# Quantising the second FFN's input in 512-column slices, shared between VectorE and ScalarE and interleaved in program order with the output matmuls

## The chip, the cores and the metric

The kernel runs on the 8 cores of one Trainium2 chip. Each core takes one of the 8 sequences of the batch, with the same weights, and the cores don't talk to each other. The metric is the device time of the slowest core in microseconds. The engines that matter here are TensorE (PE in the rows), VectorE (DVE), ScalarE (ACT) and SyncE (SP), which only issues DMAs. ScalarE issues DMAs too (ACTq).

## The reference, cut to what matters

One layer: a selective-scan attention substitute, a layernorm, a feed-forward net with quantised activations and ternary weights, and another layernorm. Per core, sequence length 2048, model width 2048, hidden width 8192.

```python
def _act_quant(x):
    scale = QB / jnp.maximum(jnp.max(jnp.abs(x), axis=-1, keepdims=True), EPS)   # QB = 127
    q = jnp.clip(jnp.round(x * scale), -QB - 1, QB) / scale
    ...
def _bitlinear(x, w):
    return jnp.einsum('bsd,od->bso', _act_quant(x), _weight_quant(w))
...
gv = _bitlinear(h, w_gv)
value, gate = jnp.split(gv, 2, axis=-1)
u = value * jax.nn.silu(gate)
out = _bitlinear(u, w_out)
return residual + out
```

The change is about the step `_act_quant(u)`: each of the 8192 x 2048 values of u is multiplied by its token's scale and rounded to an integer of at most 127 in size. The scale needs the maximum over all 8192 hidden channels, so rounding can begin only when all of u is there.

## The kernel before

Activations lie with channels on the 128 partitions and tokens along the free dimension: a hidden chunk `j` (of `HC` = 64) is a tile of 128 x 2048, and `ts` (of `NTS` = 4) names a slice of `TS` = 512 tokens. The program runs in stages, one after the other: the scan, the mean of the weights, the first layernorm and quantisation (token slices of 512), the first FFN matmul with u as its result (u goes to DRAM as `u_sp`, f32), the ternary `w_out` (to DRAM as `qo_sp`, bf16), then the two stages that the change touches.

**Quantising u (lines 1140 to 1202, "Q2" below).** A loop over the 64 chunks, whole tiles of 128 x 2048. SyncE loads `u_sp[j]` (1 MB) into one of two halves of `ub`, and waits before each load until chunk j-2 is finished (`tok_q2f`), so the next chunk's load runs under the current chunk. VectorE multiplies by the scale `s2b`; ScalarE takes Sign and Abs; VectorE peels the rounded size bit by bit (`emit_peel`, line 53: seven times a comparison into `tq` and a subtraction from `rq`), then one multiplication and one subtraction give the integer `q2t` in bf16. ScalarE's queue stores it to `q2_sp` in DRAM.

**The output matmul and layernorm ("F2" below, from line 1245).** A loop over the four token slices. SyncE first waits that all of q2 is stored, then loads per step `qo_r` (256 KB) and `q_r` (`q2_r`, 128 KB) into rings of four; TensorE runs 2 x 64 steps of 8 matmuls (line 1286) into all of PSUM; ScalarE copies the results to `o_ts`; SyncE loads the residual `lbuf` (16 DMAs); then comes a tail: VectorE scales and adds (two passes over 128 x 8192), TensorE and ScalarE make the layernorm's sums, VectorE the statistics, ScalarE copies the broadcast mean and 1/std (`tok_bc6c`), VectorE makes two more passes over 128 x 8192 (`tok_out`), and ScalarE's queue stores 16 pieces to `outT`. The next slice's matmuls wait for `tok_bc6c` only, so they run beside the last two passes and the stores.

**What sets the order.** Each engine, SyncE included, executes its own instructions strictly in the order in which the program emits them. Each compute instruction of VectorE and ScalarE is followed by a wait of that engine for its own result; dependences on others are further waits placed before the instruction. A wait holds up all that is behind it on the same engine:

```python
def call(*a, **kw):
    r = f(*a, **kw)
    s.inc(r)
    e.wait_ge(s.h, s.n)
    return r
```

## Time and profile before

| | us |
|---|---|
| median of the 2 timed runs (8724.84 and 8746.99) | 8735.91 |
| the profiled execution | 8729.62 |
| span of its slowest core, core 0, first to last instruction | 8728.1 |
| spans of the 8 cores | 8684.9 to 8728.1 |
| VectorE busy | 4400.0 (50%) |
| TensorE busy | 3306.6 (38%) |
| ScalarE busy | 2212.0 (25%) |

The profile is of one execution, on its slowest core. All times within it count from that core's first instruction. An engine's busy share is an average over stages with different limits, so it says little by itself. The stages can be told apart by time: Q2 runs from 5006 to about 7417 us, F2 from there to the end at 8728 us. "Idle before, releaser" in a row is the time that the engine stood still before the instruction and what ended that.

### The profile page before, as it was taken

The numbers are of one execution on the slowest core, as the hardware profiler recorded it, in microseconds if no ns is written. First come the engines' busy times: TensorE is split into PE (matmuls) and PEld (weight loads), VectorE is DVE, ScalarE is ACT, GpSimd is POOL, SyncE is SP. The second block draws the span as 40 slices with busy tenths as digits, with TensorE's granted clock in tenths as the row PEclk, the third lists the DMA queues.
The fourth block names the chain that finished last, engine by engine and source line by source line (L and its number), as shares of the span: only waits on it lengthen the run. The fifth ranks groups of instructions, "written<-read, shape, count | busy, mean of one in ns | idle before, by whom it ended". The sixth has DMA issues, their size and how long they took to land.

```text
span 8728.1 us, 45431 instructions; the slowest of 8 cores (8684.9 to 8728.1 us)
## 1 busy us (share of the span) xinstructions
PE 3306.6 (38%) x13138; PEld 1338.2 (15%) x13138; DVE 4400.0 (50%) x2983; ACT 2212.0 (25%) x2199; POOL 44.1 (1%) x87
## 2 busy tenths in 40 slices
PE   2100102102399988898820000000000000977966
PEld 0000000000144433333310000000000000422422
DVE  4500174674644444444433488888888888011011
ACT  3544323123234343343455401111011110001010
POOL 1000000000000000000000000000000000000000
PEclk7555555555688899999965555555555555988988
DMA  7775301001122222222245301111111110755754
GB/s 172 268 255 187 116 19 39 27 12 36 58 92 97 92 102 92 97 97 92 102 147 200 134 36 43 43 43 43 38 42 43 43 43 35 216 172 161 218 165 147
DMA packets 316760, 887.05 MB, mean 102 GB/s; under 512 B 43872, under 2 KB 109408, under 8 KB 267360
## 3 DMA queue, kind: packets, MB, share of 16 engines
q1 hardware_dynamic: 249264, 704.77, 25.3%
q10 hardware_dynamic: 55296, 167.80, 4.9%
q0 software_dynamic: 11952, 11.57, 1.0%
q8 instruction: 107, 1.75, 0.1%
q14 instruction: 141, 1.16, 0.0%
HBM read 727.79 MB, written 167.77 MB: 103 GB/s over the span
## 4 chain that ended last, share of the span: by engine, by line
DVE 44%; PE 19%; ACT 19%; DMA 11%; issue 4%; ACTq 1%; DVEq 1%; SPq 1%; POOL 0%; POOLq 0%
DVE rq L80 12%; PE pout L1286 9%; DVE tq L80 8%; DMA wmean<-wgvt 4%; PE pvg L1012 4%; PE pvg L1017 4%; ACT wqt L80 4%; ACT wqs L80 4%; DMA wmean<-woutT 3%; DVE res L80 3%; DVE paby L80 3%; ACT wabs L80 2%; DMA q_r<-q_sp 2%; DVE Mx L80 2%; DVE ub L80 2%
## 5 line engine op out<-in xcount | busy, mean ns | idle before, releaser
L1286 PE MATMUL pout<-q_r,qo_r 128*128 128x512 bf16 x4096 | 919.7, 387 | 2492.1 <-DMA q_r<-q_sp 2455.1
L1012 PE MATMUL pvg<-q,qwv 128*128 128x512 bf16 x4096 | 1056.4, 417 | 308.9 <-DVE qwg L80 159.1
L80 DVE TENSOR_TENSOR rq<-rq,tq 128x2048 f32<-128x2048 f32 x448 | 1027.0, 2292 | 48.1 <-DVE tq L80 1.8
L1017 PE MATMUL pvg<-q,qwg 128*128 128x512 bf16 x4096 | 984.1, 396 | 0.0
L1286 PEld LDWEIGHTS pout<-q_r,qo_r 128*128 128x128 bf16 x4096 | 403.3, 99 | 3012.8 <-issue 2559.9
L80 DVE TENSOR_SCALAR tq<-rq 128x2048 f32<-128x2048 f32 x448 | 549.6, 1227 | 309.4 <-ACT rq L80 268.0
L80 ACT ACTIVATE sgq<-ub 128x2048 bf16<-128x2048 f32 x64 | 122.2, 1909 | 2118.3 <-DVE ub L80 2118.3
L1012 PEld LDWEIGHTS pvg<-q,qwv 128*128 128x128 bf16 x4096 | 428.6, 105 | 902.0 <-issue 615.0
L80 ACT ACT_TABLE_LOAD x78 | 100.1, 1283 | 1753.3 <-PE pout L1286 536.5
L80 DVE TENSOR_TENSOR o_ts<-o_ts,c2b 128x8192 f32<-128x8192 f32 x4 | 34.8, 8691 | 985.6 <-DMA lbuf<-ln_sp 985.6
L80 ACT ACTIVATE wabs<-wmean 128x2048 f32<-128x2048 f32 (+1 forms) x256 | 379.6, 1483 | 457.6 <-DMA wmean<-wgvt 245.2
L1017 PEld LDWEIGHTS pvg<-q,qwg 128*128 128x128 bf16 x4096 | 414.2, 101 | 527.5 <-issue 189.6
L80 DVE SCALAR_TENSOR_TENSOR qo_t<-wqt,wqs 128x1024 bf16<-128x1024 f32 x128 | 156.9, 1226 | 345.3 <-ACT wqs L80 345.3
L80 DVE TENSOR_REDUCE redW<-accW 128x1 f32<-128x128 f32 x2 | 0.6, 286 | 643.8 <-ACT wabs L80 643.7
L80 ACT ACTIVATE wqt<-wld,sgv 128x2048 f32<-128x2048 f32 x128 | 256.3, 2002 | 251.3 <-DVE qwv L80 163.8
L80 DVE SCALAR_TENSOR_TENSOR qwv<-wqt,wqs 128x2048 bf16<-128x2048 f32 x64 | 146.7, 2292 | 312.8 <-ACT wqs L80 308.0
L80 ACT ACTIVATE sg_t<-gc_t 128x512 f32<-128x512 f32 x256 | 161.2, 630 | 564.2 <-DVE gc_t L80 564.2
L80 DVE SCALAR_TENSOR_TENSOR qwg<-wqt,wqs 128x2048 bf16<-128x2048 f32 x64 | 146.7, 2292 | 275.6 <-ACT wqs L80 275.6
L80 DVE TENSOR_TENSOR Mx<-Mx,au_t 128x512 f32<-128x512 f32 x256 | 177.2, 692 | 213.4 <-ACT au_t L80 213.4
L80 DVE TENSOR_TENSOR sg_t<-sg_t,c1b 128x512 f32<-128x512 f32 x256 | 177.2, 692 | 211.9 <-ACT sg_t L80 211.9
L80 ACT ACTIVATE au_t<-u_r 128x512 f32<-128x512 f32 x256 | 161.2, 630 | 469.5 <-DVE u_r L80 469.5
L80 ACT ACTIVATE wqs<-wld,sgv 128x2048 bf16<-128x2048 f32 x128 | 256.2, 2002 | 12.4 <-ACT wqt L80 0.8
(141 smaller groups left out, 3349.1 us busy)
## 6 DMA issues: line engine op xcount, KB each, us to landing
wmean<-wgvt SPq DMA_DIRECT2D x128, 1024.0 KB, 5.6
wld<-wgvt SPq DMA_DIRECT2D x128, 1024.0 KB, 5.2
qo_r<-qo_sp SPq DMA_DIRECT2D x512, 256.0 KB, 3.1
wmean<-woutT SPq DMA_DIRECT2D x128, 512.0 KB, 4.3
u_sp<-u_r ACTq DMA_DIRECT2D x64, 1024.0 KB, 3.8
wo_r<-woutT SPq DMA_DIRECT2D x128, 512.0 KB, 3.5
ub<-u_sp SPq DMA_DIRECT2D x64, 1024.0 KB, 4.7
q_r<-q_sp SPq DMA_DIRECT2D x512, 128.0 KB, 3.6
```

The costliest lines, as they stand in the source:

```text
L80: r = f(*a, **kw)
L1012: t.matmul(pvg[:, 2 * q * TS:(2 * q + 1) * TS], qwv[:, r * 2048 + k * 128:r * 2048 + (k + 1) * 128], q1[:, (ts * DC + k) * TS:(ts * DC + k ...
L1017: last = t.matmul(pvg[:, (2 * q + 1) * TS:(2 * q + 2) * TS], qwg[:, r * 2048 + k * 128:r * 2048 + (k + 1) * 128], q1[:, (ts * DC + k) * TS ...
L1286: last = t.matmul(pout[:, d * TS:(d + 1) * TS], qo_r[:, (i % 4) * 1024 + d * 128:(i % 4) * 1024 + (d + 1) * 128], q2_r[:, (i % 4) * TS:(i ...
```

## The change

The stage Q2 over whole chunks is taken out. In its place `emit_q2_slice(ts)` quantises one slice of 512 tokens, all 64 chunks of it, and the body of the F2 loop becomes `emit_f2_slice(ts)`. The program emits them in the order q2(0), q2(1), f2(0), q2(2), f2(1), q2(3), f2(2), f2(3), and every engine's instructions stand in this order.

Within q2(ts) two chunks are worked on together as two lanes. Each has one half of `ub2`, `zt2`, `mq2` and `q2c` (128 x 512 each). VectorE multiplies each lane by the scale; then there are eight levels k, in each of which ScalarE takes the Sign of the remainder plus 0.5 (`bias=pbh[:]`, a tile of 128 x 1) and VectorE adds `HYB_S[k]` times that sign to the remainder (`scalar_tensor_tensor`). A last `scalar_tensor_tensor` per lane gives the integer plus 0.5, ScalarE subtracts 0.5 and converts to bf16 (Copy), and its queue stores 128 KB to `q2_sp`. `vfin[nj]` is the count of VectorE's last instruction on a lane; the load of the chunk two further on, into the same half of `ub2`, waits for it. In F2, SyncE waits for the stores of this slice instead of all (`rQ2S`), and for a list of events `BND` of earlier stages. The diff, cut:

```diff
--- before.py
+++ after.py
     c2b = sb(nc.sbuf_tensor("c2b", [128, S], F32))
+    s2b = sb(nc.sbuf_tensor("s2b", [128, S], F32))
+    pbh = sb(nc.sbuf_tensor("pbh", [128, 1], F32))
+    pbm = sb(nc.sbuf_tensor("pbm", [128, 1], F32))
...
-    ub = f15.enter_context(nc.sbuf_tensor("ub", [128, 2 * S], F32))
-    rq = f15.enter_context(nc.sbuf_tensor("rq", [128, S], F32))
-    tq = f15.enter_context(nc.sbuf_tensor("tq", [128, S], F32))
-    sgq = f15.enter_context(nc.sbuf_tensor("sgq", [128, S], BF16))
-    q2t = f15.enter_context(nc.sbuf_tensor("q2t", [128, 2 * S], BF16))
...
-    @blk.sync
-    def _(s):
-        for j in range(HC):
-            s.wait_ge(*TOK[("usp", j)])
-            if j < 2:
-                s.wait_ge(sV.h, tok_s2row)
-                s.wait_ge(sA.h, tok_c2b)
-                for h_, v_ in tok_qosp:
-                    s.wait_ge(h_, v_)
-            else:
-                s.wait_ge(sV.h, tok_q2f(j - 2))
-            ub_toks[j] = rUB.inc(j, s.dma_start(out=ub[:, (j % 2) * S:(j % 2 + 1) * S],
-                                                in_=u_sp[j]))
-
-    @SCA
-    def _(sc):
-        for j in range(HC + 1):
-            if j < HC:
-                sc.wait_ge(sV.h, tok_q2y(j))
-                if j >= 1:
-                    sc.wait_ge(sV.h, tok_q2f(j - 1))
-                sc.activation(out=sgq[:], in_=ub[:, (j % 2) * S:(j % 2 + 1) * S],
-                              func=AF.Sign)
-                sc.activation(out=rq[:], in_=ub[:, (j % 2) * S:(j % 2 + 1) * S],
-                              func=AF.Abs)
-            if j >= 1:
-                jj = j - 1
-                sc.wait_ge(sV.h, tok_q2f(jj))
-                rQ2S.inc(jj, sc.dma_start(out=q2_sp[jj],
-                                          in_=q2t[:, (jj % 2) * S:(jj % 2 + 1) * S]))
-    tok_q2abs_end = sA.n
-    @VEC
-    def _(v):
-        v.wait_ge(sA.h, tok_c2b)
-        for j in range(HC):
-            r = j % 2
-            v.wait_ge(*ub_toks[j])
-            v.tensor_mul(out=ub[:, r * S:(r + 1) * S],
-                         in0=ub[:, r * S:(r + 1) * S], in1=s2b[:])
-            v.wait_ge(sA.h, q2_a0 + 2 * (j + 1))
-            emit_peel(v, rq[:], tq[:])
-            v.tensor_mul(out=tq[:], in0=rq[:], in1=sgq[:])
-            if j >= 2:
-                v.wait_ge(rQ2S.sems[j % 2].h, 16 * (j // 2))
-            v.tensor_sub(out=q2t[:, r * S:(r + 1) * S],
-                         in0=ub[:, r * S:(r + 1) * S], in1=tq[:])
-    assert sV.n == q2_v0 + 17 * HC, (sV.n, q2_v0)
-
-    tok_q2sp = [s.tok() for s in rQ2S.sems]
...
+    ub2 = f2b(nc.sbuf_tensor("ub2", [128, 2 * TS], F32))
+    zt2 = f2b(nc.sbuf_tensor("zt2", [128, 2 * TS], F32))
+    mq2 = f2b(nc.sbuf_tensor("mq2", [128, 2 * TS], F32))
+    q2c = f2b(nc.sbuf_tensor("q2c", [128, 2 * TS], BF16))
...
+    HYB_S = [-64.0, -32.0, -16.0, -8.0, -4.0, -2.0, -1.0, -0.5]
+
+    BND = ([(sV.h, tok_s2row), (sV.h, tok_qodone), (sA.h, tok_woq),
+            (sA.h, tok_c2b), (sLn1.h, tok_ln1_all)]
+           + [TOK[("usp", HC - 2)], TOK[("usp", HC - 1)]] + list(tok_qosp))
+
+    vfin = {}
+    ub2_toks = {}
+    q2stash = {}
+
+    def emit_q2_slice(ts):
+        vb, ab = sV.n, sA.n
+        for jj in range(HC):
+            vfin[ts * HC + jj] = vb + 20 * (jj // 2) + 19 + (jj % 2)
+        sl = slice(ts * TS, (ts + 1) * TS)
+
+        @blk.sync
+        def _(s, ts=ts):
+            for jj in range(HC):
+                nj = ts * HC + jj
+                if ts == 0:
+                    s.wait_ge(*TOK[("usp", jj)])
+                    if jj < 2:
+                        for h_, v_ in BND:
+                            s.wait_ge(h_, v_)
+                if nj >= 2:
+                    s.wait_ge(sV.h, vfin[nj - 2])
+                r = jj % 2
+                ub2_toks[nj] = rUB.inc(nj, s.dma_start(
+                    out=ub2[:, r * TS:(r + 1) * TS],
+                    in_=u_sp[jj, :, ts * TS:(ts + 1) * TS]))
+
+        @VEC
+        def _(v, ts=ts, vb=vb, ab=ab, sl=sl):
+            for pj in range(HC // 2):
+                for lane in range(2):
+                    jj = 2 * pj + lane
+                    v.wait_ge(*ub2_toks[ts * HC + jj])
+                    r = jj % 2
+                    v.tensor_mul(out=ub2[:, r * TS:(r + 1) * TS],
+                                 in0=ub2[:, r * TS:(r + 1) * TS],
+                                 in1=s2b[:, sl])
+                for k in range(8):
+                    for lane in range(2):
+                        r = (2 * pj + lane) % 2
+                        v.wait_ge(sA.h, ab + 18 * pj + 2 * k + lane + 1)
+                        v.scalar_tensor_tensor(
+                            out=zt2[:, r * TS:(r + 1) * TS],
+                            in0=mq2[:, r * TS:(r + 1) * TS], scalar=HYB_S[k],
+                            in1=(ub2 if k == 0 else zt2)[:, r * TS:(r + 1) * TS],
+                            op0=ALU.mult, op1=ALU.add)
+                for lane in range(2):
+                    r = (2 * pj + lane) % 2
+                    v.scalar_tensor_tensor(
+                        out=mq2[:, r * TS:(r + 1) * TS],
+                        in0=zt2[:, r * TS:(r + 1) * TS], scalar=-1.0,
+                        in1=ub2[:, r * TS:(r + 1) * TS],
+                        op0=ALU.mult, op1=ALU.add)
+        assert sV.n == vb + 20 * (HC // 2)
+
+        @SCA
+        def _(sc, ts=ts, vb=vb, ab=ab):
+            for pj in range(HC // 2):
+                for k in range(8):
+                    for lane in range(2):
+                        r = (2 * pj + lane) % 2
+                        sc.wait_ge(sV.h, vb + 20 * pj
+                                   + (1 + lane if k == 0 else 2 * k + 1 + lane))
+                        sc.activation(out=mq2[:, r * TS:(r + 1) * TS],
+                                      in_=(ub2 if k == 0 else zt2)[:, r * TS:(r + 1) * TS],
+                                      func=AF.Sign, bias=pbh[:])
+                for lane in range(2):
+                    jj = 2 * pj + lane
+                    nj = ts * HC + jj
+                    r = jj % 2
+                    sc.wait_ge(sV.h, vfin[nj])
+                    if nj >= 2:
+                        sc.wait_ge(*q2stash[nj - 2])
+                    sc.activation(out=q2c[:, r * TS:(r + 1) * TS],
+                                  in_=mq2[:, r * TS:(r + 1) * TS],
+                                  func=AF.Copy, bias=-0.5)
+                    q2stash[nj] = rQ2S.inc(r, sc.dma_start(
+                        out=q2_sp[jj, :, ts * TS:(ts + 1) * TS],
+                        in_=q2c[:, r * TS:(r + 1) * TS]))
+        assert sA.n == ab + 18 * (HC // 2)
 
...
+    def emit_f2_slice(ts):
...
-            for h_, v_ in tok_q2sp:
-                s.wait_ge(h_, v_)
+            for l_ in range(2):
+                s.wait_ge(rQ2S.sems[l_].h, 16 * (HC // 2) * (ts + 1))
             for h_, v_ in tok_qosp:
                 s.wait_ge(h_, v_)
+            if ts == 0:
+                for h_, v_ in BND:
+                    s.wait_ge(h_, v_)
             for dg in range(2):
                 for j in range(HC):
...
             if prev_next_ok is not None:
                 t.wait_ge(sA.h, prev_next_ok)
+            else:
+                t.wait_ge(sA.h, tok_c2b)
...
+    emit_q2_slice(0)
+    for ts in range(NTS):
+        if ts + 1 < NTS:
+            emit_q2_slice(ts + 1)
+        emit_f2_slice(ts)
```

## Rows read from the trace of the kernel before

**Rows 1.** Windows: length; busy of PE, PEld, DVE, ACT, POOL; clock; DMA share; GB/s.

```profile
5006.00:7420.00 2414.00, 0.00 (x0) 0.00 (x0) 2016.56 (x1088) 245.68 (x130) 0.00 (x0) 0.50 0.11 42
7420.00:7655.00 235.00, 226.13 (x1023) 100.23 (x1024) 0.00 (x0) 5.96 (x9) 0.00 (x0) 0.98 0.77 215
7728.00:7976.00 248.00, 231.57 (x1022) 101.39 (x1023) 17.38 (x2) 6.05 (x10) 0.00 (x0) 0.95 0.75 217
```

**Rows 2.** Groups of instructions by shape: busy us, mean ns; idle before, releasers.

```profile
L80 DVE TENSOR_TENSOR rq<-rq,tq 128x2048 f32<-128x2048 f32 x448 | 1027.0, 2292 | 48.1 <-DVE tq L80 1.8
...
L80 DVE TENSOR_SCALAR tq<-rq 128x2048 f32<-128x2048 f32 x448 | 549.6, 1227 | 309.4 <-ACT rq L80 268.0 <-DVE rq L80 0.9
...
L80 DVE SCALAR_TENSOR_TENSOR qwg<-wqt,wqs 128x2048 bf16<-128x2048 f32 x64 | 146.7, 2292 | 275.6 <-ACT wqs L80 275.6
```

**Rows 3.** Instructions on tile ub: duration min/median/max, first and last start.

```profile
L80 DVE TENSOR_TENSOR ub<-ub,s2b x64: 2291/2292/2293, 5011.1 to 7377.0; 128x2048 f32<-128x2048 f32 x64
```

**Rows 4.** SyncE's waits: for what, us in total, times, longest.

```profile
SPq L1162 <- DVE q2t L80: 2304.0, 62, 42.4
```

**Rows 5.** Timeline (start, us, engine), SyncE first to F2's matmuls, final passes and stores.

```profile
5006.22 43.80 SPq L1163 DMA_DIRECT2D ub<-u_sp  x3
...
7420.15 20.22 PE L1286 MATMUL pout<-q_r,qo_r 128*128 128x512 bf16 x85 [2417.36 <-DMA q_r<-q_sp]
...
7728.34 23.90 PE L1286 MATMUL pout<-q_r,qo_r 128*128 128x512 bf16 x96 [2.89 <-ACT rstd2b L80]
...
7736.99 8.69 DVE L80 TENSOR_TENSOR o_ts<-o_ts,rstd2b 128x8192 f32<-128x8192 f32 x1
...
7745.76 14.12 ACTq L1431 DMA_DIRECT2D outT<-o_ts  x16
...
8373.54 2.72 PE L1286 MATMUL pout<-q_r,qo_r 128*128 128x512 bf16 x6 [2.89 <-ACT rstd2b L80]
```

**Rows 6.** Groups by shape, 512 columns; the third has a 1-column tile as bias.

```profile
L80 DVE TENSOR_TENSOR Mx<-Mx,au_t 128x512 f32<-128x512 f32 x256 | 177.2, 692 | 213.4 <-ACT au_t L80 213.4
...
L80 ACT ACTIVATE au_t<-u_r 128x512 f32<-128x512 f32 x256 | 161.2, 630 | 469.5 <-DVE u_r L80 469.5
...
L80 ACT ACTIVATE scr<-scr,epsc 1x512 f32<-1x512 f32 x12 | 8.6, 720 | 0.1
```

**Rows 7.** Timeline, a two-buffer exchange between ScalarE and VectorE in the first quantisation.

```profile
1157.00 0.63 ACT L80 ACTIVATE paby<-hbuf 128x512 f32<-128x512 f32 x1 [0.23 <-DVE m1t L80]
1157.08 0.69 DVE L80 TENSOR_TENSOR m1t<-m1t,paby 128x512 f32<-128x512 f32 x1 [0.17 <-DVE m1t L80]
1157.86 0.63 ACT L80 ACTIVATE paby<-hbuf 128x512 f32<-128x512 f32 x1 [0.23 <-DVE m1t L80]
```

**Rows 8.** Timeline, ScalarE alone: copies without a further wait, squares with one.

```profile
7656.58 4.62 ACT L80 COPY o_ts<-pout 128x512 f32<-128x512 f32 x7 [0.37 <-ACT o_ts L80]
...
7701.44 10.72 ACT L80 ACTIVATE sqb<-o_ts 128x512 bf16<-128x512 f32 x14 [14.21 <-PE pout L1376]
```

**Rows 9.** Timeline, additions whose two-buffer loads wait for the addition two before.

```profile
1001.99 0.69 DVE L80 TENSOR_TENSOR res<-res,xr 128x512 f32<-128x512 f32 x1 [2.39 <-DMA xr<-xT]
...
1005.85 0.69 DVE L80 TENSOR_TENSOR res<-res,xr 128x512 f32<-128x512 f32 x1 [2.23 <-DMA xr<-xT]
```

**Rows 10.** Tile xr: time from issue to landing of its 64 loads.

```profile
DMA to landing us min/median/max: 2.6/3.0/4.1
```

**Rows 11.** DMA issues: line, engine, count, KB each, median us to landing.

```profile
ub<-u_sp SPq DMA_DIRECT2D x64, 1024.0 KB, 4.7
...
xr<-xT SPq DMA_DIRECT2D x64, 256.0 KB, 3.0
```

**Rows 12.** Timeline of ScalarE: 16 stores, then the next block's table load and work.

```profile
1091.55 9.02 ACTq L677 DMA_DIRECT2D ln_sp<-res  x16
1100.60 1.28 ACT L80 ACT_TABLE_LOAD   x1 [26.72 <-issue]
1101.90 2.13 ACT L80 ACTIVATE sqb<-res 128x512 bf16<-128x512 f32 x3
```

**Rows 13.** Timeline of ScalarE: a copying instruction followed by Silu in one block.

```profile
94.70 0.59 ACT L80 CAST zbf<-pz 128x512 bf16<-128x512 f32 x1 [2.87 <-DVE zf L80]
97.36 0.60 ACT L80 ACTIVATE gsil<-pg 128x512 f32<-128x512 f32 x1 [2.08 <-PE pg L259]
```

More of the change, by code:

```diff
@@ L239, in _ @@
         v.memset(yacc[:], 0.0)
+        v.memset(pbh[:], 0.5)
+        v.memset(pbm[:], -0.5)
     tok_init = sV.n
@@ L1250, in build_program @@
     prev_mm_end = None
-    for ts in range(NTS):
+    def emit_f2_slice(ts):
+        nonlocal prev_next_ok, prev_res2, prev_mm_end
         f2_m0 = sMM.n
@@ L1307, in _ @@
             s.wait_ge(sLn1.h, tok_ln1_all)
+            if ts == 0:
+                for h_, v_ in BND:
+                    s.wait_ge(h_, v_)
             if prev_res2 is not None:
```

31 lines of the change are left out of this document (removed).

## The prediction

> **What bounds the kernel now.** I read the windows first. They cut the time that the change touches in two. In Q2, 2414 us, TensorE does nothing at all, VectorE is busy 2017 us and ScalarE 246 us. In a slice of F2 it is the reverse: 226 of 235 us are TensorE's, in the first slice, and the granted clock is 0.98 (2.4 GHz) where Q2 had 0.50 (1.2 GHz) [rows 1]. So Q2 is VectorE's stage. Its groups by shape say what fills it: seven comparisons of 1.23 us and seven subtractions of 2.29 us per chunk, and three more passes of 2.29 us [rows 2]. The 64 chunks follow each other every (7377.0 - 5011.1) / 63 = 37.55 us [rows 3]. SyncE's waits show that no load is late there: SyncE waits 2304 us in total for VectorE to free a buffer, never the other way round in the steady state [rows 4]. After Q2 comes F2, four times in turn. The first matmul of slice 0 starts at 7420.15, that of slice 1 at 7728.34, that of slice 3 at 8373.54, and the span ends at 8728.1 [rows 5].
>
> **Does anything overlap after the change?** The emission order q2(1), f2(0), q2(2), f2(1), q2(3), f2(2), f2(3) looks as if q2(ts+1) ran beside f2(ts). Follow SyncE, which keeps its order. The loads of f2(0) stand behind the 64 loads of q2(1), and each of these waits for the chunk two before it (`vfin`). So f2(0)'s matmuls get their first data when the last pair of q2(1) has been loaded. In return q2(2) is behind f2(0)'s whole tail on VectorE and on ScalarE. The two stages still alternate; only the last of the 32 pairs of q2(1), q2(2) and q2(3) lies beside the following matmuls. The question is therefore what 32 pairs cost against 16 old chunks, 16 x 37.55 = 601 us.
>
> **One pair, step by step.** VectorE has 20 passes of 512 columns, at 0.692 us each [rows 6]; the `scalar_tensor_tensor` costs as much as the plain multiplication at 2048 columns, 2292 ns [rows 2], so I take 0.692 for it too. ScalarE has 16 Signs at 0.72 us (0.630 for an ACTIVATE, 0.720 for one with a column as bias) and 2 Copies at 0.63 [rows 6]. What lies between instructions decides as much. The exchange paby/m1t has this very pattern, two buffers, each engine waiting for itself and for the other: VectorE repeats every 0.86 us, which is 0.69 and a gap of 0.17 [rows 7]. The hand-over from VectorE to ScalarE takes 0.09 (1157.77 to 1157.86). ScalarE with only its own wait has a gap of (4.62 - 7 x 0.585) / 6 = 0.09, and with one more wait, already fulfilled, (10.72 - 14 x 0.63) / 13 = 0.14 [rows 8]. A level then costs:
> - ScalarE: 2 x (0.72 + 0.14) = 1.73 us;
> - VectorE: 2 x (0.69 + 0.17) = 1.72 us;
> - one lane's own chain: 0.72 + 0.10 + 0.69 + 0.09 = 1.61 us.
>
> The dearest rules: 1.73, a value that the chain bounds from below (1.61) and the gap of 0.23 that ScalarE shows in the exchange [rows 7] from above (1.90). A pair from its first multiplication: that one and the hand-over 0.79; seven levels 12.1; then the last Sign of lane 1, 0.86 + 0.72, hand-over 0.10, VectorE's last level step 0.69, gap 0.10 and the final pass of lane 0, 0.69. Together 16.05 us. Only now may lane 0's next load go, since both halves of `ub2` are in use: the prefetch that Q2 had is gone. The additions `res<-res,xr` show the price of such a loop with loads of the same shape (256 KB, rows of 2 KB): an addition ends at 1002.68 and the one that needs the freed buffer starts at 1005.85 [rows 9], 3.17 us, of which landing is 3.0 (2.6 to 4.1) [rows 10]. So a pair takes 16.05 + 3.17 = 19.2 us. ScalarE's Copies and its two DMA issues fall into these 3.2 us and the next multiplication: 2 x (0.63 + 0.33) and gaps are 2.3 us, out of 4.0. If that cover were gone they would cost up to 2.3 us a pair.
>
> A slice is 32 x 19.2 = 614 us against 601 before: VectorE's work fell (20 x 0.692 = 13.8 us a pair, 443 us a slice, against 2017 / 4 = 504), but the levels alternate at ScalarE's pace and the load lies bare.
>
> The Trainium skill, in "DMA: Bandwidth & Descriptors", section "Anatomy of one DMA", gives a fixed 2.0 us plus the bytes at 436 GB/s. By that rule, which speaks against cutting 1 MB loads into bare 256 KB ones, a load is an estimated 2.6 us and the total 50 us less than mine. The rows have 3.0 for 256 KB and 4.7 for 1 MB [rows 11], so they decide, and the 2.6 agrees with the smallest landing.
>
> **The sum, in the trace's time.**
> - q2(0) starts as Q2 did, SyncE at 5006.2 [rows 5]; with 3.2 for the load, the first multiplication is at 5009.4.
> - 63 pairs, to the start of the last pair of q2(1): 1209.6. Each block of ScalarE begins with a table load of 1.28 us [rows 12], two of them: 2.6. Now 6221.6.
> - f2(0)'s loads are issued behind lane 1's last load, some 2 us before this, and need 3 to 4 us: first matmul 1.8 later, 6223.4.
> - f2(0) from first matmul to the end of the fourth pass on VectorE, as before: 7745.68 - 7420.15 = 325.5 [rows 5]. Now 6548.9.
> - q2(2) cannot start its Signs then: ScalarE first issues 16 stores, and in front of the same pattern of the first layernorm 9.0 us of issues and 1.3 of table load went by [rows 12]. Against the normal hand-over that is 9.6 us. Then 31 pairs, 595.2: 7153.7.
> - f2(1): 1.8 + 325.5. q2(3): 9.6 + 595.2. First matmul of f2(2) 1.8 later: 8087.6.
> - f2(2) to f2(3)'s first matmul: 308.2, as slice 0 [rows 5]. The old slices 1 to 3 began beside the stores of `outT` (248 us for slice 1's matmuls against 235 [rows 1]); in f2(1) and f2(2) that contention goes. The low clock at their start is already in slice 0's 308.2, since it too followed an idle TensorE.
> - f2(3) as before: 8728.1 - 8373.5 = 354.6. Span 8750.
>
> That is 22 us, 0.25%, above the span of before. The sum is against that execution (8729.6 us); carried to the median of the runs, 8735.9 x 8750 / 8728.1 = 8758 us. The gains (most of a pair hidden three times, 3 x 17.4 = 52 us; two slices without contention, 645.2 - 2 x 308.2 = 29) are eaten by the quantising itself, 128 pairs and their starts against 2414, 49 us, and by passes and stores that no longer lie beside matmuls, 2 x (17.3 + 9.6) = 54.
>
> **Rivals.** Two per cent of 8736 us is 175 us, about what a measurement of this kernel can tell from no change. With 128 pairs that is 1.2 us a pair above mine for slower, and 1.5 below for faster.
> 1. The second wait is hidden and loads land at their quickest. Then the lane's chain rules, 1.61 a level, and loads take 2.6: 0.9 + 0.4 = 1.3 us a pair, -166: 8592. For it: the two engines are within 0.12 us a level of it. Against it: the gap of 0.17 stands in each step of the exchange, with both waits fulfilled [rows 7]. Chance 8%, with half-way cases.
> 2. Slower: Sign and Copy don't share a table, so ScalarE loads one before the first Copy and one before the next pair's first Sign. The first is covered by the load of u, the second comes after the multiplication that it waits for: 1.28 us bare, and little slack left, 165 us: 8923. It decides on slower from 1.2 us a pair. Against it: a copying instruction is followed by Silu without a load in one block [rows 13], and Sign, Abs and Silu alternate in the FFN stage. For it: the new Copy is an ACTIVATE with a bias, which the trace never shows. Chance 5%. The page "ScalarE: Activation LUTs" of the Trainium skill, section "Table sets: the hidden batching unit", has copy among the cheap functions in every set, which speaks against this rival too; that these rows agree for Silu is all that the trace bears out.
> 3. Dearer: the loads of u suffer from the stores beside them and from the other cores and land after up to 4.1 us, the longest of xr [rows 10], or ScalarE's gap is 0.23 as in the exchange [rows 7] and not 0.14. That is up to 1.1 us a pair for the one, 8899, and up to 2 x 8 x 0.09 = 1.4 for the other, 8938; both in full, 9080. Against it: the 0.23 there is ScalarE waiting for a slower partner, and here it is the slower one. Chance 15%, half of it beyond 2%.
> 4. The overlap works after all and three slices' matmuls vanish under quantising: 3 x 235 = 705, 8053. Against it stands SyncE's order, which nothing in the diff breaks. Chance 2%.
>
> The forecast itself: 70%. The likeliest's 8758 is the predicted time. The range 8660 to 8900 leaves out rivals 2 and 4, most of 1 and the far half of 3, about 2 in 10 in all. Faster by over 2%: 2% from rival 4 and 3% from rival 1 with cheaper passes. Slower by over 2%: rival 2 with 5% and 8% of rival 3. Within 2%: 82%.
>
> **What the profile after would show.** Starts of the multiplication on `ub` every 19.2 us within q2; per level two Signs of 0.72 and two VectorE passes of 0.69 in 1.73 us; about 3.1 us of VectorE idle before each pair, released by DMA; TensorE idle for about 580 us three times and busy in four blocks of 235 us, the first starting near 6223; no table loads inside a block. Wrong would be my pair if the Sign with a bias is dearer than 0.72 or the load dearer than 3.2, and the frame if matmuls run beside more than one pair.

## The result and the profile after

| | before | after |
|---|---|---|
| median (us), lowest to highest | 8744.5, 8711.6 to 8848.8 | 8907.4, 8878.2 to 9041.9 |
| executions | 10 | 11 |
| ratio of times, 95% interval | | 1.019, 1.0156 to 1.0225 |
| span of core 0 in the profiled execution | 8728.1 | 8875.9 |

The kernel became slower by 163 us, seven times the 22 us of the forecast. The time lies just above the range (8900) and 1.9% above before; the interval of the ratio reaches past 2%, so it isn't settled whether the loss is more or less than 2%. The sign is the one of the sum. The ratio leaves out executions in which one die ran at a lower clock and took longer, such as the one of 9041.9; the medians and the extremes are those of all. The account below goes by core 0, the core whose rows the prediction rests on.

First the frame. Timeline of TensorE on core 0 after (start, us, engine, operation, idle before): the first matmuls of the four F2 slices.

```profile
6292.49 1.01 PE L1294 MATMUL pout<-q_r,qo_r 128*128 128x512 bf16 x2 [1278.64 <-ACT mq L80]
...
7254.91 1.44 PE L1294 MATMUL pout<-q_r,qo_r 128*128 128x512 bf16 x3 [657.19 <-ACT mq L80]
...
8218.28 1.01 PE L1294 MATMUL pout<-q_r,qo_r 128*128 128x512 bf16 x2 [658.72 <-DMA q_r<-q_sp]
...
8528.31 1.01 PE L1294 MATMUL pout<-q_r,qo_r 128*128 128x512 bf16 x2 [2.89 <-ACT rstd2b L80]
```

TensorE is idle before the first matmul for 1279 us (from the stage ahead on, so this holds q2(0) and q2(1)) and before the second and third for 657 and 659 us. The windows of core 0 (columns as in [rows 1]) say the same in another way: 388 us in the middle of q2(2), then the matmuls of f2(0), f2(1) and f2(2).

```profile
6862.00:7250.00 388.00, 0.00 (x0) 0.00 (x0) 266.61 (x386) 246.56 (x347) 0.00 (x0) 0.50 0.14 39
...
6292.00:6530.00 238.00, 226.39 (x1023) 100.29 (x1024) 12.31 (x18) 17.83 (x26) 0.00 (x0) 0.97 0.75 215
7254.90:7492.90 238.00, 226.43 (x1024) 100.30 (x1024) 11.76 (x17) 18.16 (x27) 0.00 (x0) 0.98 0.74 216
8218.00:8456.00 238.00, 227.50 (x1023) 100.34 (x1024) 12.28 (x18) 17.79 (x26) 0.00 (x0) 0.97 0.75 214
```

In the matmuls' 238 us VectorE is busy for 12 us: 17 or 18 passes, the rest of one pair. Nothing else of q2 overlaps. SyncE's waits (core 5, the slowest) say who holds the order together: it spends 2617.5 us waiting for the final passes before it may load the next chunk.

```profile
SPq L1189 <- DVE mq L80: 2617.5, 248, 114.6
```

Then the pair. Tile `ub` on core 0 (its multiplications from first to last, what the engines' idle time before its instructions ended with, and the landing of its loads):

```profile
L80 DVE TENSOR_TENSOR ub<-ub,s2b x256: 691/692/695, 5020.5 to 8217.0; 128x512 f32<-128x512 f32 x128
...
  DMA ub<-u_sp: 421.6, 248
...
DMA to landing us min/median/max: 3.0/3.5/7.7
```

One pair of core 0, timeline, from the multiplication of its lane 0 to that of the next pair:

```profile
5081.94 0.69 DVE L80 TENSOR_TENSOR ub<-ub,s2b 128x512 f32<-128x512 f32 x1 [2.78 <-DMA ub<-u_sp]
5082.72 0.72 ACT L80 ACTIVATE mq<-ub,pbh 128x512 f32<-128x512 f32 x1 [2.36 <-DVE ub L80]
5083.06 0.69 DVE L80 TENSOR_TENSOR ub<-ub,s2b 128x512 f32<-128x512 f32 x1 [0.43 <-DMA ub<-u_sp]
...
5084.71 12.02 ACT L80 ACTIVATE mq<-zt,pbh 128x512 f32<-128x512 f32 x14
...
5085.65 0.69 DVE L80 SCALAR_TENSOR_TENSOR zt<-mq,zt 128x512 f32<-128x512 f32 x1 [0.17 <-DVE zt L80]
5086.51 0.69 DVE L80 SCALAR_TENSOR_TENSOR zt<-mq,zt 128x512 f32<-128x512 f32 x1 [0.17 <-DVE zt L80]
...
5097.68 1.49 DVE L80 SCALAR_TENSOR_TENSOR mq<-zt,ub 128x512 f32<-128x512 f32 x2
5098.45 1.11 SPq L1191 DMA_DIRECT2D ub<-u_sp  x2
5098.52 0.63 ACT L80 ACTIVATE q2c<-mq 128x512 bf16<-128x512 f32 x1 [1.78 <-DVE mq L80]
5099.22 0.35 ACTq L1244 DMA_DIRECT2D q_sp<-q2c  x1
5099.73 0.63 ACT L80 ACTIVATE q2c<-mq 128x512 bf16<-128x512 f32 x1 [0.59 <-DVE mq L80]
5100.44 0.33 ACTq L1244 DMA_DIRECT2D q_sp<-q2c  x1
5101.85 0.69 DVE L80 TENSOR_TENSOR ub<-ub,s2b 128x512 f32<-128x512 f32 x1 [2.69 <-DMA ub<-u_sp]
```

The pair takes 5101.85 - 5081.94 = 19.91 us. Lane 1's multiplication begins 1.12 us after lane 0's, released by its own load and not by lane 0's end (that would be 0.86). The passes repeat every 0.865. The final pass of lane 0 ends at 5098.37, the load is issued at 5098.45, and 3.48 us after the freed buffer the next multiplication starts. Over the pairs of core 0 inside slices (without the first pairs of q2(2) and q2(3), whose Signs start 10 us late behind the stores) the mean is 20.14 us a pair, of which 3.60 are from the freed buffer to the multiplication, with lane 1 on average 1.06 behind lane 0. The other cores have 20.15 to 20.24.

Groups of the page after, core 5 (busy us, mean ns; idle before, releaser), and at the end the page's count of instruction fetches (packets, MB):

```profile
L80 ACT ACTIVATE mq<-zt,pbh 128x512 f32<-128x512 f32 x1792 | 1293.5, 722 | 280.6 <-DVE zt L80 24.5
L80 DVE SCALAR_TENSOR_TENSOR zt<-mq,zt 128x512 f32<-128x512 f32 x1792 | 1242.0, 693 | 325.6 <-DVE zt L80 258.5
...
L80 ACT ACT_TABLE_LOAD x81 | 103.9, 1283 | 1743.1 <-PE pout L1294 469.4
...
L80 DVE TENSOR_TENSOR ub<-ub,s2b 128x512 f32<-128x512 f32 x256 | 177.2, 692 | 434.3 <-DMA ub<-u_sp 433.3
...
L80 ACT ACTIVATE q2c<-mq 128x512 bf16<-128x512 f32 x256 | 161.3, 630 | 309.5 <-DVE mq L80 307.8
...
q14 instruction: 237, 1.94, 0.1%
```

The Sign with a column as bias takes 722 ns, the scaled addition 693, the Copy 630: the three durations that the prediction took from other instructions [rows 6] hold to 3 ns. The table loads went from 78 to 81, one for each of the three blocks that ScalarE has more; none stands inside a block.

### The profile page after: what moved, and what is told of

Same layout as the page of the kernel before. It is cut to its first block, busy times and chain, and to the rows that moved or that the text cites. A ratio compares the mean times of both kernels' runs of the same rounds, so it can differ in the third digit from the quotient of the medians.

```text
span 8963.6 us, 57819 instructions; the slowest of 8 cores (8839.0 to 8963.6 us)
## 1 busy us (share of the span) xinstructions
PE 3331.3 (37%) x13138; PEld 1344.3 (15%) x13138; DVE 4158.0 (46%) x4457; ACT 3611.0 (40%) x4378; POOL 44.1 (0%) x87
## 4 chain that ended last, share of the span: by engine, by line
DVE 39%; ACT 21%; DMA 15%; PE 13%; issue 7%; DVEq 1%; ACTq 1%; SPq 1%; POOL 0%; POOLq 0%
DVE zt L80 13%; PE pout L1294 10%; DMA ub<-u_sp 5%; ACT wqt L80 4%; ACT wqs L80 4%; DMA wmean<-wgvt 4%; ACT mq L80 3%; DMA wmean<-woutT 3%; DVE res L80 3%; DVE paby L80 3%; DVE Mx L80 2%; ACT wabs L80 2%; DVE sg_t L80 2%; DVE gc_t L80 2%; DVE u_r L80 2%
## 5 line engine op out<-in xcount | busy, mean ns | idle before, releaser
L1294 PE MATMUL pout<-q_r,qo_r 128*128 128x512 bf16 x4096 | 1004.1, 413 | 2653.3 <-DMA q_r<-q_sp 2622.4
L80 ACT ACTIVATE mq<-zt,pbh 128x512 f32<-128x512 f32 x1792 | 1293.5, 722 | 280.6 <-DVE zt L80 24.5
L80 DVE SCALAR_TENSOR_TENSOR zt<-mq,zt 128x512 f32<-128x512 f32 x1792 | 1242.0, 693 | 325.6 <-DVE zt L80 258.5
L1016 PE MATMUL pvg<-q,qwv 128*128 128x512 bf16 x4096 | 1030.8, 410 | 367.3 <-DVE u_r L80 206.7
L1021 PE MATMUL pvg<-q,qwg 128*128 128x512 bf16 x4096 | 941.6, 384 | 0.0
L1294 PEld LDWEIGHTS pout<-q_r,qo_r 128*128 128x128 bf16 x4096 | 425.6, 104 | 3236.0 <-issue 3007.4
L80 DVE TENSOR_TENSOR ub<-ub,s2b 128x512 f32<-128x512 f32 x256 | 177.2, 692 | 434.3 <-DMA ub<-u_sp 433.3
L80 ACT ACTIVATE mq<-ub,pbh 128x512 f32<-128x512 f32 x256 | 184.7, 722 | 350.2 <-DVE ub L80 349.1
L80 ACT ACTIVATE q2c<-mq 128x512 bf16<-128x512 f32 x256 | 161.3, 630 | 309.5 <-DVE mq L80 307.8
```

The costliest lines, as they stand in the source:

```text
L1016: t.matmul(pvg[:, 2 * q * TS:(2 * q + 1) * TS], qwv[:, r * 2048 + k * 128:r * 2048 + (k + 1) * 128], q1[:, (ts * DC + k) * TS:(ts * DC + k ...
L1021: last = t.matmul(pvg[:, (2 * q + 1) * TS:(2 * q + 2) * TS], qwg[:, r * 2048 + k * 128:r * 2048 + (k + 1) * 128], q1[:, (ts * DC + k) * TS ...
L1294: last = t.matmul(pout[:, d * TS:(d + 1) * TS], qo_r[:, (i % 4) * 1024 + d * 128:(i % 4) * 1024 + (d + 1) * 128], q2_r[:, (i % 4) * TS:(i ...
```

## The sum against the trace, step by step

| step, core 0 | forecast (us) | measured | difference |
|---|---|---|---|
| start of the first multiplication | 5009.4 | 5020.5 | +11.1 |
| from there to f2(0)'s first matmul (63 pairs) | 1214.0 | 1272.0 | +58.0 |
| f2(0) to f2(1) (f2's 325.5, 9.6, 31 pairs, 1.8) | 932.1 | 962.4 | +30.3 |
| f2(1) to f2(2), the same | 932.1 | 963.4 | +31.3 |
| f2(2) to f2(3) | 308.2 | 310.0 | +1.8 |
| f2(3) to the end | 354.6 | 347.6 | -7.0 |
| span | 8750 | 8876 | +126 |

Three rows carry the difference, and they are those with pairs: 58.0 / 63 = 0.92, 30.3 / 31 = 0.98, 31.3 / 31 = 1.01 us a pair. The frame between them is right to 2 us. The first row belongs to the stages ahead: in the kernels of the experiments, which share them, the same multiplication on core 0 starts between 4970.9 and 5026.5. So one term was mis-sized, the pair of 19.2, and 125 exposed pairs multiply it: 120 of the 126 us. The late start (+11.1) and the short last slice (-7.0) largely cancel, by luck. The experiments ask what its 0.92 us are, and whether the order of the queues really is what keeps the overlap away.

## The experiments

Two things are asked. Is it SyncE's order that keeps the stages apart, or something that would hold in any order? And which of these makes a pair dearer than its rows: the stores beside the loads, the place that the loads read from, a pause of the queues ahead of them, or the pair's own two loads beside each other? Diffs are against the changed kernel, cut to the core. "Wait" means the time from lane 0's final pass to the next multiplication, and "pair" the mean distance of two pairs' first multiplications within slices, again without the two late first pairs. Both are for core 0 unless said otherwise. Experiments 5 and 8 to 11 were executed once each, so their times say little and their pairs carry the argument.

**1. The stores later and from another engine.** The two stores of a pair run beside the two loads of the next. Here GpSimd issues them, five levels into the next pair.

```diff
-                    q2stash[nj] = rQ2S.inc(r, sc.dma_start(
+        @blk.gpsimd
+        def _(g, ts=ts, ab=ab):
...
+                    g.wait_ge(sA.h, ab + 18 * pj + 17 + lane + (5 if pj < HC // 2 - 1 else 0))
+                    tok = rQ2S.inc(r, g.dma_start(
```

> The changed kernel, with the two stores of each pair moved: GpSimd issues them when ScalarE has finished five Signs of the next pair, so that they no longer fly beside the loads of u. In the changed kernel a pair takes 20.1 us where I had forecast 19.2: lane 0's multiplication starts 3.4 to 3.6 us after the buffer is free (forecast 3.2) and lane 1's 1.0 to 1.3 us after lane 0's (forecast 0.86). Theory S (the stores delay the loads): landing of the loads falls from 3.5 to 3.0 us, a pair to 19.2, the whole by 128 x 0.9 = 115 us. Theory L (the loads of u are dearer in themselves, or wait for those of the other cores): landing and pair stay as they are, the whole within 20 us of the changed kernel.

Measured: 8894.9 us, ratio 1.018 (1.013 to 1.022). The pair is 19.96, the wait 3.56, lane 1 now starts 0.91 behind (0.87 in the median, which is no lateness at all). So with both loads in flight the stores cost 0.2 us of 0.92, and they did it mainly to lane 1's load. As the whole cause they fall.

**2. Four buffers for `u`.** The loads wait for the chunk four before, so that one pair is loaded while the other is quantised.

```diff
-    ub2 = f2b(nc.sbuf_tensor("ub2", [128, 2 * TS], F32))
+    ub2 = f2b(nc.sbuf_tensor("ub2", [128, 4 * TS], F32))
...
-                if nj >= 2:
-                    s.wait_ge(sV.h, vfin[nj - 2])
+                if nj >= 4:
+                    s.wait_ge(sV.h, vfin[nj - 4])
```

> The changed kernel with four buffers for u instead of two, and a load that waits for the chunk four before it: the next pair's loads fly under the present pair. If the bare load is what the change paid with, VectorE no longer waits for DMA and a pair falls from 20.1 to about 17.6 us (ScalarE: last Sign, two Copies, two DMA issues, next Sign), which is 128 x 2.5 = 320 us less than the changed kernel, ratio to the kernel before about 0.98. If other waits take its place (ScalarE's issues, stores that hold up the Copies), the pair stays above 18.5 us and less than 200 us are gained.

Measured: 8641.2, ratio 0.987 (0.984 to 0.991), 266 us under the changed kernel, and 254 under experiment 3, which ran on the same chip. The pair is 18.03 instead of the expected 17.6. Tile `ub` of this kernel: the engine waits on a load twice in the whole run.

```profile
  DMA ub<-u_sp: 25.1, 2
```

What came in its place stands in the timeline of core 0, between two pairs:

```profile
5413.20 0.69 DVE L80 TENSOR_TENSOR ub<-ub,s2b 128x512 f32<-128x512 f32 x1 [0.17 <-DVE mq L80]
5413.60 0.63 ACT L80 ACTIVATE q2c<-mq 128x512 bf16<-128x512 f32 x1 [0.59 <-DVE mq L80]
5414.07 0.69 DVE L80 TENSOR_TENSOR ub<-ub,s2b 128x512 f32<-128x512 f32 x1 [0.17 <-DVE ub L80]
5414.31 0.33 ACTq L1246 DMA_DIRECT2D q_sp<-q2c  x1
5414.74 1.59 ACT L80 ACTIVATE mq<-ub,pbh 128x512 f32<-128x512 f32 x2 [0.51 <-ACT q2c L80]
5415.56 0.69 DVE L80 SCALAR_TENSOR_TENSOR zt<-mq,ub 128x512 f32<-128x512 f32 x1 [0.80 <-ACT mq L80]
```

The multiplication is ready at 5413.89, but ScalarE begins the Sign only at 5414.74, behind two Copies and two DMA issues. These are the 2.3 us that the prediction hid under the bare load. The cover is gone, and part of them shows: 0.80 us that VectorE waits for ScalarE instead of 0.17.

**3. No interleaving in the emission order.** All four q2 slices, then all four f2 slices.

```diff
-    emit_q2_slice(0)
     for ts in range(NTS):
-        if ts + 1 < NTS:
-            emit_q2_slice(ts + 1)
+        emit_q2_slice(ts)
+    for ts in range(NTS):
         emit_f2_slice(ts)
```

> The changed kernel with one thing undone, the emission order: q2(0) to q2(3) first, then f2(0) to f2(3). It tells what the interleaving is worth. By the prediction's terms it loses three hidden pairs (+55 us), has the passes and stores beside matmuls again (-54) and their contention (+29): 30 us slower than the changed kernel. If the interleaving hid matmuls beyond one pair it would be some hundred us slower; if alternating costs more than it hides, it is faster than the changed kernel.

Measured: 8895.2, ratio 1.020 (1.015 to 1.026), which can't be told from the changed kernel's 1.019. The interleaved emission is worth nothing, as the prediction said. All that it could hide, a pair three times, goes, by the forecast's account (which no run splits up), for the passes and stores that it puts on the path.

**4. The order merged by hand.** With four buffers, and with SyncE's list written so that after each pair's two loads come those of four of the 128 matmul steps of the slice before. ScalarE empties the first half of `pout` after pair 17.

```diff
+                if mg and jj % 2 == 1:
+                    pj = jj // 2
+                    if pj == 0:
+                        f2_load_waits(s, tf)
+                    for i in range(4 * pj, 4 * pj + 4):
+                        f2_load(s, tf, i, f2_m0, m_end, toks)
```

> Four buffers as in the run before, and SyncE's order written out so that the two stages really overlap: after the two loads of each pair of q2(ts+1) SyncE issues four of the 128 steps of f2(ts), ScalarE copies the first half's results out after pair 17, and the residual is loaded in good time. If SyncE's order was what kept the stages apart, TensorE's 235 us vanish under quantising in three of four slices, and the whole comes to 5006 + 4 x 563 + 3 x 95 + 350 = 7890 us, ratio 0.90. If the two stages slow each other (DMA share, or the clock), q2's pairs get longer than 17.6 us beside matmuls and the ratio stays above 0.93.

Measured: 7955.8, ratio 0.910 (0.908 to 0.913). That is 685 us under experiment 2; three slices of matmuls are 3 x 235 = 705. Window of core 0 over the pairs of one merged slice:

```profile
5560.00:6130.00 570.00, 281.67 (x1003) 112.08 (x1024) 433.70 (x628) 406.20 (x572) 0.00 (x0) 0.75 0.45 139
```

TensorE, VectorE and ScalarE are busy in the same stretch, TensorE with a whole slice, and the pair is 18.16 against experiment 2's 18.03, so the stages hardly slow each other. The work was free to overlap, and the order of the queues kept it apart: SyncE's first of all, since nothing reaches TensorE without it. ScalarE's copies of the first half were moved too; by the waits TensorE could otherwise run only the first 64 of its 128 steps, but no run splits the two moves. Rival 4's 8053 was about the right price for an overlap that this emission order can't give.

**5. Another source for the loads.** `ub2` is filled from `xT`, with the same shape and count. What is quantised is then other data.

```diff
-                    in_=u_sp[jj, :, ts * TS:(ts + 1) * TS]))
+                    in_=xT[(jj % DC) * 128:(jj % DC + 1) * 128, ts * TS:(ts + 1) * TS]))
```

> The changed kernel, but the loads into ub2 read the same shape (128 rows of 2 KB, 8 KB apart) from the input xT instead of from u_sp, so it quantises other data and its output is not the reference's. In the row on which my load price rested, those were loads from xT. Moving the stores away took only 0.2 to 0.4 of the 0.9 us that a pair is dearer than forecast. Theory U (u_sp, an internal tensor in DRAM, is slower to read): landing falls from 3.5 to 3.0 us and a pair from 20.1 to about 19.6. Theory N (the source does not matter, the loads collide with stores and with each other): landing 3.4 to 3.5, pair 20.1 as in the changed kernel.

Measured: 8916.1 beside 8729.9 for the kernel before. The pair is 20.07, the median landing 3.5. With the very source of [rows 10], whose loads landed in 3.0, they take 3.5 here. The source is not it.

**6. Whole chunks.** The same levels and engines on 2048 columns, q2 first and f2 after it. The slicing is undone; besides, there are three buffers where the changed kernel has two, so that the loads are mostly hidden (VectorE is idle 0.7 us in the mean before a multiplication).

```diff
+QW = 2048
...
-    ub2 = f2b(nc.sbuf_tensor("ub2", [128, 2 * TS], F32))
+    ub2 = f2b(nc.sbuf_tensor("ub2", [128, 3 * QW], F32))
```

> The change's sign-and-add levels without its slices: whole chunks of 2048 columns, two lanes, three buffers for u, all of the quantising first and then the four slices of F2, as in the kernel before. It separates the two parts of the change, the new arithmetic and the slicing. A pass of VectorE over 2048 columns takes 2.29 us and a gap of 0.17, so a pair of chunks costs 20 x 2.46 = 49 us against 4 x 20.1 = 80 in the changed kernel and 75 in the kernel before. With a third buffer one of the two loads is hidden and the other (4.8 us) mostly not: 49 to 54 us, 32 pairs are 1575 to 1730 us against 2414: the whole at 7900 to 8050, ratio 0.90 to 0.92. If the fixed cost of an instruction was not what the slices cost, and the levels themselves are the burden, it stays above 0.95.

Measured: 7970.2 (7917.4 to 8053.3), ratio 0.910 (0.899 to 0.920). Window of core 0 over nearly all of Q2:

```profile
5000.00:6600.00 1600.00, 9.58 (x11) 2.82 (x9) 1459.94 (x638) 1151.02 (x579) 0.00 (x0) 0.50 0.17 62
```

Q2 begins at 5021 and ends its last pass at 6607, 1586 us; before it took 2414. So the new arithmetic (eight Signs and eight scaled additions per chunk in place of seven comparisons, seven subtractions and a product), with the third buffer, is a gain of some 800 us, and cutting it into 512 columns with two buffers spends more than all of it. A pass takes 2.29 us on 2048 columns and 0.692 on 512, four of which are 2.77, and each has its own gap.

**7. Slices of 1024 columns, merged.** Four buffers, q2 in two slices; f2(0) and f2(1) lie beside the second.

```diff
+QW = 1024
...
+    q2_part(0, 0, HP)
+    q2_part(1, 0, 9, g0)
+    mm_steps(0, 0, HC)
+    evac(0, 0)
...
+    f2_plain(2)
+    f2_plain(3)
```

> Both lessons together: slices of 1024 columns (two of them), four buffers for u, and under the second slice SyncE's order written so that f2(0), its tail and f2(1) run beside and between the pairs; f2(2) and f2(3) follow. A pair takes 20 x (1.226 + 0.17) = 27.9 us, 64 of them 1787. Sum: 5006 + 3 + 1787 + 95 (tail 0) + 75 (tail 1) + 321 + 355 = 7642 us, ratio 0.875. If matmuls beside the quantising slow its pairs (DMA, clock) or waits at the part boundaries pile up, it comes to 7750 or more.

Measured: 7724.2, ratio 0.881 (0.874 to 0.889), the fastest kernel of this study. Window of core 0 in the second slice:

```profile
5890.00:6370.00 480.00, 256.60 (x1024) 106.12 (x1024) 393.11 (x322) 337.08 (x301) 0.00 (x0) 0.76 0.54 158
```

It carries a whole F2 slice of matmuls while VectorE is busy 82% of the time. It hides fewer matmuls than experiment 4 (two slices instead of three), but its passes of 1.225 us pay the fixed part of a pass half as often.

**8. More traffic between the pairs.** Four further loads of 256 KB a pair, into a buffer that nobody reads, so that the queues are never idle for long.

```diff
+                if jj % 2 == 1:
+                    for k in (1, 3, 5, 7):
+                        s.wait_ge(sA.h, ab + 18 * (jj // 2) + 2 * k + 1)
+                        s.wait_ge(sK.h, sK.n)
+                        sK.inc(s.dma_start(out=kbuf[:],
```

> The changed kernel with four more loads of 256 KB per pair into a buffer that nobody reads, issued by SyncE while the levels run, the last one just before the pair ends. The source is not it (reading xT left landing at 3.5 us), and taking the stores away gave only 0.1 us of the 0.4 us by which lane 0's load is late. What still differs from the additions of the first layernorm is that those loads came every 2 us and these come after 16 us in which the queue is at rest. Theory I (a load after a rest costs more): landing of the loads into ub2 falls to 3.0 to 3.2 us, the wait from free buffer to multiplication from 3.5 to 3.2, the whole by 40 to 60 us. Theory C (it is traffic, of this core or its neighbours): more traffic makes landing worse, 3.6 or more, and nothing is gained.

Measured: 8986.5 beside 8725.2. The pair is 20.39, the wait 3.80, the landing 3.7. A load is not dear because its queue had been idle; more traffic makes it dearer.

**9. The same with the stores moved as in experiment 1.**

```diff
+                        sK.inc(s.dma_start(out=kbuf[:],
...
-                    q2stash[nj] = rQ2S.inc(r, sc.dma_start(
...
+                    tok = rQ2S.inc(r, g.dma_start(
```

> Both: the stores moved to GpSimd and to the next pair's fifth level, and the four extra loads per pair. If rest and stores are the two causes, the wait is 3.2 us, lane 1 follows lane 0 by 0.9, and a pair takes 19.4 us, its body with VectorE's own pace (16.2) and its occasional longer gaps (0.2) included. If the pair stays at 19.8 to 20.0 as with the stores moved alone, the rest is not a cause.

Measured: 8934.0. The pair is 19.83 to 20.39 over the cores, the wait 3.28 to 3.84. In experiment 1 they are 19.74 to 20.07 and 3.25 to 3.66, so the added loads don't help here either, and the pause ahead of a load is no cause.

**10. One load a pair.** Lane 1's load is left out; lane 1 multiplies lane 0's half.

```diff
+                if r == 1:
+                    ub2_toks[nj] = ub2_toks[nj - 1]
+                    continue
...
-                                 in0=ub2[:, r * TS:(r + 1) * TS],
+                                 in0=ub2[:, 0:TS],
```

> The changed kernel with lane 1's loads of u left out (its multiplication reads lane 0's half, so half of the quantised data is not the reference's). Filling the rest of the queue made the wait longer, not shorter, so the idea of a cost after a rest is dropped. Left is that the pair's own transfers get in each other's way. Theory P (lane 1's load and the store slow lane 0's load): the wait for lane 0 falls from 3.5 to about 3.2 us; lane 1 then follows by 0.86, and a pair takes about 19.7 us. Theory F (256 KB cost 3.4 to 3.6 us here whatever flies beside them, as a matter of the eight cores together): the wait stays at 3.4 to 3.6 us.

Measured: 8820.9 beside 8725.6. The pair is 19.68, the wait 3.31, lane 1 is 0.87 behind, the landing 3.1.

**11. One load a pair, and the stores late.**

```diff
+                if r == 1:
+                    ub2_toks[nj] = ub2_toks[nj - 1]
+                    continue
...
-                    q2stash[nj] = rQ2S.inc(r, sc.dma_start(
...
+                    tok = rQ2S.inc(r, g.dma_start(
```

> The same, lane 1's loads left out, with the stores moved to GpSimd and into the next pair's fifth level: lane 0's load is then alone in its core's queues. Theory P: the wait is 3.1 to 3.2 us, as in the additions of the first layernorm. Theory F: still 3.4 or more.

Measured: 8810.8 beside 8725.6. The pair is 19.51, the wait 3.13 (median 3.06), the landing 2.9. Tile `ub` of this kernel on core 0:

```profile
DMA to landing us min/median/max: 2.8/2.9/9.7
```

With one load in flight and no store beside it, the wait is what the rows promised (3.17 from [rows 9]). The steps 3.60, 3.31, 3.13 give the second load 0.3 and the stores 0.2 us on core 0; as means over the eight cores they are 3.53, 3.35 and 3.18, 0.2 each. The shares depend on the order in which the transfers are taken away: without the stores alone (experiment 1) the wait is 3.56 on core 0 and 3.46 in the mean.

**12. Four buffers and the stores from GpSimd.** Experiments 1 and 2 together, to price ScalarE's two DMA issues.

```diff
-    ub2 = f2b(nc.sbuf_tensor("ub2", [128, 2 * TS], F32))
+    ub2 = f2b(nc.sbuf_tensor("ub2", [128, 4 * TS], F32))
...
-                    q2stash[nj] = rQ2S.inc(r, sc.dma_start(
...
+                    tok = rQ2S.inc(r, g.dma_start(
```

> Four buffers for u, and the stores issued by GpSimd in the next pair. With four buffers a pair took 18.1 to 18.2 us where I had expected 17.6; between two pairs VectorE waits 0.80 us for the first Sign, which stands behind two Copies and two DMA issues on ScalarE. If these two issues (0.33 us each and their waits) are what is in the way, a pair falls to 17.4 to 17.5 us (20 passes at 0.863 us and 0.2 of longer gaps), 128 x 0.7 = 90 us less than with four buffers alone, ratio 0.977. If GpSimd's issues disturb VectorE, its passes get longer than 0.69 us and nothing is gained.

Measured: 8530.9, ratio 0.976 (0.971 to 0.981). The pair is 17.37, 0.66 less than in experiment 2, which is about two issues of 0.33 us. Timeline of core 0 between two pairs:

```profile
5414.29 0.63 ACT L80 ACTIVATE q2c<-mq 128x512 bf16<-128x512 f32 x1 [1.80 <-DVE mq L80]
5415.11 0.69 DVE L80 TENSOR_TENSOR ub<-ub,s2b 128x512 f32<-128x512 f32 x1 [0.17 <-DVE mq L80]
5415.12 0.63 ACT L80 ACTIVATE q2c<-mq 128x512 bf16<-128x512 f32 x1 [0.20 <-DVE mq L80]
5415.90 1.59 ACT L80 ACTIVATE mq<-ub,pbh 128x512 f32<-128x512 f32 x2
5415.98 0.69 DVE L80 TENSOR_TENSOR ub<-ub,s2b 128x512 f32<-128x512 f32 x1 [0.17 <-DVE ub L80]
5416.84 0.69 DVE L80 SCALAR_TENSOR_TENSOR zt<-mq,ub 128x512 f32<-128x512 f32 x1 [0.17 <-DVE ub L80]
```

VectorE goes from pair to pair here without a wait longer than 0.17: 20 passes x 0.866 = 17.3 us is the floor of a pair of this width, and this kernel stands on it to 0.1. The edit also moves the stores away from the loads, but with four buffers VectorE waits for a load only twice in either kernel, so that the gain is the issues'.

## Why the prediction was right in its frame and wrong in its size

**Serialisation: right, and shown.** "The two stages still alternate" was read from SyncE's order. Experiment 3 takes the interleaving away and loses nothing. Experiment 4 keeps experiment 2's work and changes the order of the queues, and wins 685 us. Only one pair lies beside each F2 block, as the 17 or 18 VectorE passes in its 238 us show.

**The F2 blocks: right.** f2(1) and f2(2) have lost the contention with the `outT` stores: their matmuls take 238 us, as slice 0's, and not the 248 of slice 1 in [rows 1]. The late start of q2(2) and q2(3), 9.6 us behind the stores and the table load, fits: f2(0) to f2(1) less 31 pairs of 20.14 is 338.1, against 325.5 + 9.6 + 1.8 = 336.9. The last slice came out 7 us shorter than before, which the prediction had taken as equal: its 1024 matmuls take 246.6 us on core 0 and took 252.9, the longest of all cores before, so the 354.6 was long for its own trace (the other seven cores had 347 to 351). TensorE's idle time was put at "about 580 us"; it is 658. This was a slip beside the sum, whose own terms give 932.1 - (308.2 - 2.9) = 626.8; the other 30 us are the dearer pairs.

**The durations: right.** The Sign with bias, the scaled addition and the Copy came out as read. Rival 2, a table load between Sign and Copy, did not happen. Rival 1, a hidden second wait, neither: the 0.17 stands in nearly every pass. ScalarE's gap is (12.02 - 14 x 0.722) / 13 = 0.15, not rival 3's 0.23.

**The failing step: "So a pair takes 16.05 + 3.17 = 19.2 us".** It takes 20.14 = 16.54 + 3.60. The 0.92 divide like this:

- *The load, +0.43.* The prediction wrote that the additions on `xr` "show the price of such a loop with loads of the same shape". They show that of a load whose companions don't hurt. Here lane 1's load and the two stores of the pair fly beside it. With all three taken away (experiment 11) the wait is 3.13, with the stores back 3.31, with everything 3.60. That the three together are the cause is shown; how they share it is not fixed, as experiment 1 shows. This is rival 3's mechanism, "the loads of u suffer from the stores beside them", with a companion that the rival forgot, the pair's own second load. It got 15%, and its bound for this part was 1.1 us.
- *The pace, +0.16.* The prediction let "the dearest" rule, ScalarE with 1.73 a level. The two engines are in fact tied: VectorE passes every 0.866, so a level is 1.732. But then the path ends on VectorE, which has 18 passes in a row ahead of lane 0's final one: 18 x 0.866 + 0.692, less 0.07 for the one gap of 0.10, is 16.21. In the pairs where lane 1 isn't late and no gap is long, the body is 16.22 (the median of experiments 10 and 11), against 16.05. The longer path through the same instructions was there to be counted.
- *Long gaps and a late lane 1, +0.33.* Some passes start 0.52 us after the one before instead of 0.17, with all that they wait for done. On core 0, between 5020 and 6280, 27 of 877 gaps in the chain of `zt` are over 0.3 us: 14 are VectorE's own, over 0.5, and 13, of 0.34 to 0.39, come where ScalarE is late. The kernels with one load, which have no late lane, show their price as a mean of 16.37 for the body against a median of 16.22, 0.15 a pair. Two of them:

```profile
5065.42 0.69 DVE L80 SCALAR_TENSOR_TENSOR zt<-mq,zt 128x512 f32<-128x512 f32 x1 [0.53 <-DVE zt L80]
...
5108.03 0.69 DVE L80 SCALAR_TENSOR_TENSOR zt<-mq,zt 128x512 f32<-128x512 f32 x1 [0.17 <-DVE zt L80]
5109.24 0.69 DVE L80 SCALAR_TENSOR_TENSOR zt<-mq,zt 128x512 f32<-128x512 f32 x1 [0.53 <-DVE zt L80]
```

  What is left between 16.37 and 16.54, 0.17, is lane 1, whose multiplication waits for its own load, 1.06 us behind lane 0 instead of 0.86.

**The other price of the load.** The Trainium skill, in "DMA: Bandwidth & Descriptors", section "Anatomy of one DMA", made an estimated 2.6 us of a load of 256 KB. The fastest of after landed in 3.0 and the median in 3.5, so the trace lies further from it than before. That section of the Trainium skill gives its figures for DMAs that GpSimd issues, which the prediction left unsaid; these loads are SyncE's. Nothing in the sum hung on them.

**The range.** 8660 to 8900 counted rival 3 to its half. What it missed was that three small excesses, each of 0.16 to 0.43 us, could add up where 125 repeats multiply them: 0.92 us a pair is 115 us. The term that is multiplied most deserved the widest interval, and its bounds (loads that land after up to 4.1 us in [rows 10]) were known.

**What stays open.** Why two `xr` loads at a time land in 3.0 us and two `ub` loads without stores late in 3.3 (experiment 1) is not settled; experiment 5 only excludes the source. The cause of the long gaps isn't either, but the traces show what they go by. VectorE's own gaps over 0.5 us recur every 128 of its instructions, waits included, which is every 44 passes, with some missing: 43.8 us apart in after (the two rows with 0.53 above), 38.3 in experiment 12, 109 on the 2048 columns of experiment 6, and at the same spacing in the other kernels of this study and on cores 3 and 5 of after. So they go by the place in the instruction stream and not by time or by traffic. The trace that the prediction read had them too: eight gaps of 0.46 to 0.53 us in Q2, 128, 384 or 512 instructions apart. A cost of fetching instructions would fit this, but that it is the cause is not shown: the fetches of the page (141 packets before, 237 after, 147 in experiment 6) were changed by no run alone.

## What to carry to other kernels

On a queue that keeps the order of the program, the order of emission is the overlap: to interleave two stages by calling their emitters alternately does nothing here, because each puts all its loads in one run (8907 us against 8895 in experiment 3). Merge the loads step by step (here worth 685 us). When work is cut into narrower slices, price the fixed part of each instruction (a VectorE pass of 512 columns costs 0.866 us with its gap, a quarter of a 2048-column one 0.62), and the prefetch that goes with the buffers: two further buffers were worth some 260 us, and moving two DMA issues a pair off the busy engine another 85 (128 x 0.66) to 110 (the medians). A load's price must be read from rows in which as much is in flight beside it as there will be.
